# A decoder layer on one core: the output projection, the second norm and the FFN as one unrolled pipeline, and the attention outputs divided as they leave PSUM

## The chip, the core and the metric

One core of a Trainium2 chip runs the whole layer in one launch. The metric is device time in microseconds: the median of 3 runs is 2385.4 us (2385.02, 2385.40 and 2389.25 us).

## What is computed

Sixteen batches of 112 tokens, 256 wide (1792 tokens in all), go through a decoder layer with the norm after each part. The middle part is cross attention: 8 heads of width 128, with 375 keys in each batch, but heads are split off after batches and tokens are flattened, so every token sees all 6000 keys.

```python
x = layernorm(x + attn(x, Wq, Wk, Wv, Wo))            # 16 heads of 16, 4 key groups
q, k, v = split(x @ Wq), split(ctx @ Wk), split(ctx @ Wv)   # (8, 1792, 128), (8, 6000, 128)
sim = (q @ k.T) * 128 ** -0.5
mean = sim.mean(-1); sim = (sim - mean) * 1.5 + mean
out = merge(softmax(sim) @ v)                          # (1792, 1024)
x = layernorm(x + out @ Wout + bout)
h = gelu(x @ ternary(W1).T + b1)                       # exact gelu, 1024 wide
x = layernorm(x + h @ ternary(W2).T + b2)
```

Operands of the large products are kept as a high and a low float16 half, and a product is three matmuls (high by high, high by low, low by high); the ternary weights are exact and need two.

## The kernel before, in words

The program has three blocks (`with nc.Block()`), each with one instruction list per engine; at the end of a block all engines meet. Within a block every order and every wait is written out by hand: an instruction adds to a semaphore when it is done, and a list waits for a semaphore's value (`wait_ge`).

**Block 1, self attention and cross attention (lines 387 to 1274).** Cross attention runs over 56 groups `n` of 256 query tokens (8 heads by `NQB` = 7), each with 12 steps `s` of 512 keys. A step `f` is, on PE, the scores of step `f + LEAD` (`scores`, L404) and then the weighted sum of step `f` (`attend`, L428 to L432); on ACT, half of the casts of the exponentials (`exp_half`, L708), the copy of the scores into a ring (`keep_scores`, L701) and the exponential (`exp_full`, L718); on DVE, the subtraction of the row maximum (`subtract`, L879) and the running maximum (`running_max`, L858), which frees the two banks of the scores for PE; on POOL, the low half of the exponentials (L1201, L1203). `v` carries a column of ones, so that `attend` also sums the weights: a query tile has 129 columns in PSUM (`OW`), of which the last is its sum of weights. In step 1 of the next group ACT copies both query tiles of a group, 258 columns, to `o_buf` (`store_output`, L741), and SP writes them to DRAM (`store`, L1246), with the sums and undivided. `attend` of group `n` waits until group `n - 2` is copied.

**Block 2, output projection (lines 1287 to 1378).** It goes over 16 batches of 112 tokens, in loops with a body of two batches. SP loads a batch from DRAM into one of two buffers `raw` (8 heads by 129). DVE takes the reciprocal of the sums (L1302) and multiplies (L1305). PE turns the 8 heads (`transposes`, L1361), ACT and DVE split the result into halves (L1352 and `low`, L1311), PE multiplies by `Wout` (`project`, 24 matmuls, L1370), and DVE adds the residual (L1318) and collects statistics (L1321).

**Block 3, second norm, FFN and third norm (lines 1399 to 1545).** The statistics of all 16 batches are combined (L165, L167), ACT takes the roots (L174), and the FFN goes over 4 chunks of 448 tokens, three of them in a loop. For each of 8 parts `f` of the hidden layer PE does 4 matmuls (L1418), ACT does the gelu in float32 (L1442) and for even `f` again in float16 (L1447), for odd `f` DVE casts (L1505), and DVE makes the low half (L1507). Then PE does 16 matmuls for each batch (L1408), DVE adds the residual and collects statistics (L1471, L1475), and at the end of a chunk ACT takes a root (L1454) and DVE does the third norm (L1481 to L1490). The normalised and turned inputs of the next chunk (L179, L191, L197, L203) are made within the present one. SP stores two batches at a time (L1543). Roots and gelu need different tables on ACT, so each change is an `ACT_TABLE_LOAD`.

## Time and profile before

| | |
|---|---|
| median of 3 runs | 2385.4 us (2385.02 to 2389.25) |
| the profiled execution | 2389.25 us, span 2387.5 us |
| PE busy | 2296.9 us, 96% of the span |
| DVE busy | 2045.9 us, 86% |
| ACT busy | 1865.5 us, 78% |
| POOL busy | 1858.0 us, 78% |
| granted TensorE clock, mean | 0.991 |
| last matmul of block 1 starts | 2232.8 us from the start of the span |
| blocks 2 and 3 | the 154.5 us after that |

The span is the time from the first to the last instruction of one profiled execution; the rest of its 2389.25 us lies around it. The granted clock is a share of TensorE's full 2.4 GHz. A busy share is an average over stages with different limits, so the text reads stages apart. In rows of instructions, busy times of neighbours overlap; the distance from one start to the next is what an instruction costs its queue.

### The profile page before, as it was taken

The page shows a single profiled execution, that of the slowest core. Times are in us where ns is not written, and L with a number is a line of the kernel's source. Part 1 is how long each engine was busy: PE and PEld are TensorE (multiplying, and loading weights), DVE is VectorE, ACT ScalarE, POOL GpSimd, SP SyncE. Part 2 cuts the span into 40 slices and gives each one's busy share as a digit, 9 for nine tenths or more (in the row PEclk, how much of TensorE's full clock was granted, in tenths as well). Part 3 has the DMA queues.
Part 4 walks back from the last instruction along what each step waited for, and adds up shares of the span by engine and source line. Part 5 has one row for each costly group of instructions (what it writes and reads, how often), then busy time and mean ns, then how long its engine had stood idle before and what let it go on. Part 6 is the DMA issues. An engine that isn't in the chain of part 4 may idle for free. (4 is left out here: it accounts for less than half of the span.)

```text
span 2387.5 us, 67959 instructions
## 1 busy us (share of the span) xinstructions
PE 2296.9 (96%) x28874; PEld 2051.9 (86%) x28874; DVE 2045.9 (86%) x2237; ACT 1865.5 (78%) x2181; POOL 1858.0 (78%) x1110
## 2 busy tenths in 40 slices
PE   7988999999999999999999999999999999999787
PEld 3557998899989998999889988999899989998775
DVE  7878888988888888888878888888888888888776
ACT  4347888888888888888878888888888888888434
POOL 8744888888888898888878887889788888999101
PEclk9999999999999999999999999999999999999999
DMA  7401000000000000000000000000000000012211
GB/s 202 146 19 32 5 5 13 4 6 6 11 6 7 4 13 4 7 6 4 13 7 4 6 12 5 6 4 13 6 4 6 7 4 6 8 39 53 76 39 31
DMA packets 34869, 50.80 MB, mean 21 GB/s; under 512 B 2352, under 2 KB 27408, under 8 KB 34576
## 3 DMA queue, kind: packets, MB, share of 16 engines
q1 hardware_dynamic: 34576, 46.54, 6.7%
q8 instruction: 227, 3.72, 0.7%
q14 instruction: 66, 0.54, 0.1%
HBM read 31.01 MB, written 15.52 MB: 19 GB/s over the span
## 5 line engine op out<-in xcount | busy, mean ns | idle before, releaser
L1203 POOL TENSOR_TENSOR e_lo<-ring,e_hi 128x1024 f16<-128x1024 f32 (+1 forms) x665 | 1387.6, 2101 | 199.0 <-ACT ring L718 171.2
L858 DVE TENSOR_TENSOR run_max<-psum,run_max 128x1024 f16<-128x1024 f32 (+1 forms) x616 | 738.5, 1199 | 207.5 <-ACT ring L701 206.4
L701 ACT ACTIVATE ring<-psum 128x1024 f32<-128x1024 f32 (+1 forms) x672 | 674.3, 1004 | 198.8 <-PE psum L404 128.9
L879 DVE SCALAR_TENSOR_TENSOR ring<-ring,psum 128x1024 f32<-128x1024 f32 (+1 forms) x672 | 793.5, 1188 | 0.7 <-PE psum L636 0.7
L404 PE MATMUL psum<-qx_hi,k_hi 128*128 128x256 f16 x2632 | 717.9, 273 | 14.8 <-DVE run_max L858 5.9
L428 PE MATMUL psum<-v_main,e_hi 128*128 128x129 f16 x4032 | 718.2, 219 | 6.4 <-POOL e_lo L1203 6.4
L404 PE MATMUL psum<-qx_hi,k_lo 128*128 128x256 f16 x2632 | 717.7, 273 | 2.3 <-issue 2.3
L430 PE MATMUL psum<-v_main,e_hi 128*128 128x128 f16 x4032 | 718.7, 222 | 0.0
L404 PE MATMUL psum<-qx_lo,k_hi 128*128 128x256 f16 x2632 | 717.6, 273 | 0.0
L432 PE MATMUL psum<-v_main,e_lo 128*128 128x129 f16 x4032 | 716.7, 219 | 0.0
L718 ACT ACTIVATE ring<-ring 128x1024 f32<-128x1024 f32 (+1 forms) x672 | 696.4, 1036 | 1.3
L708 ACT ACTIVATE e_hi<-ring 128x1024 f16<-128x1024 f32 (+1 forms) x343 | 360.8, 1052 | 95.9 <-DVE ring L879 95.0
L1201 POOL CAST e_hi<-ring 128x1024 f16<-128x1024 f32 x329 | 334.2, 1016 | 120.6 <-ACT ring L718 117.2
L428 PEld LDWEIGHTS psum<-v_main,e_hi 128*128 128x128 f16 x4032 | 388.2, 96 | 14.5 <-POOL e_lo L1203 6.3
L432 PEld LDWEIGHTS psum<-v_main,e_lo 128*128 128x128 f16 x4032 | 398.4, 99 | 0.0
L430 PEld LDWEIGHTS psum<-v_main,e_hi 128*128 128x128 f16 x4032 | 391.3, 97 | 7.0
L404 PEld LDWEIGHTS psum<-qx_hi,k_hi 128*128 128x128 f16 x2632 | 257.2, 98 | 49.5 <-DVE run_max L858 13.6
L404 PEld LDWEIGHTS psum<-qx_hi,k_lo 128*128 128x128 f16 x2632 | 257.5, 98 | 30.3
L404 PEld LDWEIGHTS psum<-qx_lo,k_hi 128*128 128x128 f16 x2632 | 257.4, 98 | 27.1
L428 PE MATMUL psum<-v_tail,e_hi 128*128 128x129 f16 (+1 forms) x1232 | 219.8, 219 | 2.1 <-POOL e_lo L1203 2.1
L430 PE MATMUL psum<-v_tail,e_hi 128*128 128x128 f16 (+1 forms) x1232 | 220.1, 221 | 0.0
L432 PE MATMUL psum<-v_tail,e_lo 128*128 128x129 f16 (+1 forms) x1232 | 219.4, 218 | 0.0
(196 smaller groups left out, 2864.8 us busy)
## 6 DMA issues: line engine op xcount, KB each, us to landing
o_scratch<-o_buf SPq DMA_DIRECT2D x56, 129.0 KB, 2.9
raw<-o_scratch SPq DMA_DIRECT2D x16, 451.5 KB, 3.7
stage<-in_ctxT SPq DMA_DIRECT2D x6, 500.0 KB, 3.9
stage<-in_ctxT SPq DMA_DIRECT2D x12, 250.0 KB, 4.8
w_scratch<-wall SPq DMA_DIRECT2D x1, 2304.0 KB, 11.1
wall<-w_scratch SPq DMA_DIRECT2D x6, 384.0 KB, 4.1
x<-in_xT SPq DMA_DIRECT2D x4, 448.0 KB, 6.2
res<-in_x SPq DMA_DIRECT2D x1, 1792.0 KB, 15.5
```

The lines of the kernel that those rows point to most:

```text
L404: mm = pe.matmul(psum[:, 2 * (f % 2) + i // 2, (i % 2) * QB:(i % 2 + 1) * QB], lhsT=k[:, keys], rhs=q[:, qpar, :], start=(n == 0), stop=(n ...
L428: pe.matmul(out_t, lhsT=e_hi_f[keys, cols], rhs=v_f[keys, i, 0:OW], start=(s == 0 and i == 0 and t == 0), stop=False)
L430: pe.matmul(out_t[:, 0:DH], lhsT=e_hi_f[keys, cols], rhs=v_f[keys, i, OW:VW], start=False, stop=False)
L432: mm = pe.matmul(out_t, lhsT=e_lo_f[keys, cols], rhs=v_f[keys, i, 0:OW], start=False, stop=last_tile and t == QT - 1)
L701: a.activation(ring[:, f % SLOTS, 0:n], pair(f)[:, 0:n], ACT.Copy).then_inc(s_kept, 1)
L708: a.activation(e_hi[f % NEH][:, 0:n], ring[:, f % SLOTS, 0:n], ACT.Exp, scale=SIM_SCALE).then_inc(s_hi, 1)
L718: a.activation(slot, slot, ACT.Exp, scale=SIM_SCALE).then_inc(s_exp, 1)
L858: ins = v.tensor_tensor(run_max[:, 0:n], pair(f)[:, 0:n], run_max[:, 0:n], ALU.max)
L879: v.scalar_tensor_tensor(slot, slot, LIFT, psum[:, 6, 0:QB].unsqueeze(1).broadcast_to([P, t, QB]), ALU.add, ALU.subtract).then_inc(s_sub, 1)
L1201: g.tensor_copy(e_hi[f % NEH][:, 0:n], slot).then_inc(s_cast, 1)
L1203: g.tensor_tensor(e_lo[f % NEL][:, 0:n], slot, e_hi[f % NEH][:, 0:n], ALU.subtract).then_inc(s_lo, 1)
```

## The change

It has two parts.

**Division in block 1.** `o_buf` loses its column of sums. In step 1 of the next group DVE takes the reciprocal of both sums out of PSUM (`invert_sums`), and ACT copies the two tiles in two instructions with these as scale. The rows in DRAM are 128 columns for a head, and the reciprocal and the multiplication of block 2 are gone.

**One block in place of two.** Everything behind attention goes over 14 tiles of 128 tokens, not 16 batches of 112, without loops. `Wout`'s product, second norm, FFN and third norm of different tiles are interleaved by hand. There are 5 buffers `raw`; three loads are issued before the scores end and two right after. Residuals are added and evacuated two tiles at a time. The FFN has chunks of 4, 4, 4 and 2 tiles; `h32` has 3 buffers and `hT_hi` and `hT_lo` have 2; POOL takes the cast for odd `f` from DVE. PSUM: banks 0 and 1 for turned heads, 2 to 4 for the hidden layer, 5 for turned norms, 6 and 7 for both products.

```diff
-        raw = [at(VREG + r * 4128, f"raw{r}", [T, NH, OW], F32) for r in range(2)]
+        raw = [at(o, f"raw{r}", [P, NH, DH], F32)
+               for r, o in enumerate((VREG, VREG + 4096, WREG, KREG + 14336, KREG + 18432))]
...
                 def store_output(n):
-                    a.wait_ge(s_av, n * NGRP + NGRP)
+                    a.wait_ge(s_den, n + 1)
                     if n > 0:
                         a.wait_ge(s_od, n * 16)
-                    a.activation(o_buf[:, :, :], psum[:, 4 + n % 2, 0:QT * OW].rearrange(
-                        "p (t w) -> p t w", t=QT), ACT.Copy).then_inc(s_oev, 1)
+                    for t in range(QT):
+                        a.activation(o_buf[:, t, :], psum[:, 4 + n % 2, t * OW:t * OW + DH], ACT.Copy,
+                                     scale=o_den[:, t:t + 1]).then_inc(s_oev, 1)
...
+                def invert_sums(n):
+                    v.wait_ge(s_av, n * NGRP + NGRP)
+                    if n > 0:
+                        v.wait_ge(s_oev, n * QT)
+                    v.reciprocal(o_den[:, :], psum[:, 4 + n % 2, 0:QT * OW].rearrange(
+                        "p (t w) -> p t w", t=QT)[:, :, DH]).then_inc(s_den, 1)
...
                     ready = f + SUB_AHEAD
+                    if s == 1 and n > 0:
+                        invert_sums(n - 1)
...
                         sp.wait_ge(s_free, side_number(NBLK - 2, 0))
-                        for r in range(2):
-                            sp.wait_ge(s_od, (NBLK - NQB + 1) * 16)
-                            sp.dma_start(raw[r][:, :, :].rearrange("p h w -> p (h w)"),
-                                         o_part[r * T:(r + 1) * T, :]).then_inc(s_raw[r], 16)
+                        for i in range(3):
+                            load_tile(i)
                         sp.wait_ge(s_qk, NF_ALL)
...
+                        for i in range(3, NRAW):
+                            load_tile(i)
```

PE's list in the new block, with `up` the first product of the FFN for some `f` and `down` the second one for a pair of tiles:

```diff
+                pe.wait_ge(s_late, 48)
+                transposes(0)
+                for i in range(1, 6):
+                    transposes(i)
+                    project(i - 1)
+                transposes(6)
+                norm_transposes(0)
+                project(5)
+                transposes(7)
+                norm_transposes(1)
+                project(6)
+                for c in range(2):
+
+                    i = 4 * c + 8
+                    up(c, range(0, 4))
+                    transposes(i)
+                    project(i - 1)
+                    up(c, range(4, 8))
+                    transposes(i + 1)
+                    project(i)
+                    down(2 * c)
+                    if c == 0:
+                        transposes(i + 2)
+                    norm_transposes(2 * c + 2)
+                    project(i + 1)
+                    down(2 * c + 1)
+                    norm_transposes(2 * c + 3)
+                    if c == 0:
+                        transposes(i + 3)
+                        project(i + 2)
+                up(2, range(0, 4))
+                norm_transposes(6)
+                up(2, range(4, 8))
+                up(3, range(0, 8))
+                for p in range(4, 7):
+                    down(p)
```

The waits that matter there: `transposes(i)` for `low(i - 1)` (which frees banks 0 and 1), `project(i)` for `low(i)`, a part of `up` for the gelu three parts before it and for the low half of the normalised inputs of its whole chunk, the gelu for the low half three parts before it, `down(p)` for the low halves of its chunk.

**DVE in attention, step 1 of a group** (`qx_lo` is the low half of a later group's queries, `v_main` that of the values). Before:

```order
L846 SCALAR_TENSOR_TENSOR qx_lo<-psum,qx_hi 128x256
L879 SCALAR_TENSOR_TENSOR ring<-ring,psum 128x1024
L858 TENSOR_TENSOR run_max<-psum,run_max 128x1024
L879 SCALAR_TENSOR_TENSOR ring<-ring,psum 128x1024
L858 TENSOR_TENSOR run_max<-psum,run_max 128x1024
L879 SCALAR_TENSOR_TENSOR ring<-ring,psum 128x1024
L858 TENSOR_TENSOR run_max<-psum,run_max 128x1024
```

Now:

```order
L789 SCALAR_TENSOR_TENSOR qx_lo<-psum,qx_hi 128x256
L822 SCALAR_TENSOR_TENSOR ring<-ring,psum 128x1024
L801 TENSOR_TENSOR run_max<-psum,run_max 128x1024
L822 SCALAR_TENSOR_TENSOR ring<-ring,psum 128x1024
L801 TENSOR_TENSOR run_max<-psum,run_max 128x1024
L829 RECIPROCAL o_den<-psum 128x2
L822 SCALAR_TENSOR_TENSOR ring<-ring,psum 128x1024
L801 TENSOR_TENSOR run_max<-psum,run_max 128x1024
```

The reciprocal stands ahead of a subtraction and of a running maximum, once in each of the 56 groups. PE's and POOL's lists of attention are as before, and ACT's has two copies of 128x128 where one of 128x258 stood.

**DVE behind attention, from one chunk's last low half to the next chunk.** Before, the end of a chunk (`res` is the residual stream, `stats` and `meanvar` belong to the third norm):

```order
L1471 TENSOR_TENSOR res_71<-psum,res_71 112x256
L1475 BN_STATS stats_37325<-res_71 112x6
L1481 BN_AGGR meanvar_37326<-stats_37325 112x2 x4
L1482 ISA
L1483 TENSOR_SCALAR rstd_37327<-meanvar_37326 112x4
L1485 REGISTER_ALU
L1486 RECIPROCAL rstd_37327<-rstd_37327 112x4
L1487 REGISTER_ALU
L1490 TENSOR_SCALAR res_71<-res_71,meanvar_37326,rstd_37327 112x256 x4
```

Now, around the second chunk's low halves (`oT_lo` belongs to the projection, `bn`, `mean` and `inv` to the norms):

```order
L1538 BN_AGGR mean_37250<-bn_37248 128x2 x4
L1540 TENSOR_SCALAR inv_37252<-mean_37250 128x4
L1476 TENSOR_TENSOR oT_lo_37235<-psum,oT_hi_37233 128x1024
L1522 TENSOR_TENSOR hT_lo_37246<-h_2_37242,hT_hi_37244 128x512
L1522 TENSOR_TENSOR hT_lo_37246<-h_0_37240,hT_hi_37244 128x512
L1522 TENSOR_TENSOR hT_lo_37246<-h_1_37241,hT_hi_37244 128x512
L1522 TENSOR_TENSOR hT_lo_37246<-h_2_37242,hT_hi_37244 128x512
L1476 TENSOR_TENSOR oT_lo_37234<-psum,oT_hi_37232 128x1024
L1483 SCALAR_TENSOR_TENSOR res_74<-psum,res_74 128x512
L1487 BN_STATS bn_37247<-res_74 128x6 x2
```

The root of the third norm is no longer waited for in the place where it is asked for (L1540): the projection of later tiles and half of the next chunk's low halves stand between, and the cast has left the list.

## Rows read from the trace of the kernel before

**Rows 1.** Two stages: length, busy PE, PEld, DVE, ACT, POOL, then clock, DMA share, GB/s
```profile
320.00:1000.00 680.00, 676.25 (x8813) 622.33 (x8811) 599.89 (x587) 577.86 (x664) 578.12 (x336) 1.00 0.03 7
...
2233.00:2388.00 155.00, 122.99 (x928) 102.59 (x928) 111.00 (x250) 59.97 (x95) 12.18 (x16) 0.91 0.19 55
```
**Rows 2.** DVE and ACT in order of time, step 1 of a group in mid-attention
```profile
1129.38 1.23 DVE L858 TENSOR_TENSOR run_max<-psum,run_max 128x1024 f16<-128x1024 f32 x1 [0.24 <-ACT ring L701]
1130.52 1.21 DVE L879 SCALAR_TENSOR_TENSOR ring<-ring,psum 128x1024 f32<-128x1024 f32 x1
1132.19 1.23 DVE L858 TENSOR_TENSOR run_max<-psum,run_max 128x1024 f16<-128x1024 f32 x1 [0.45 <-ACT ring L701]
...
1132.99 0.38 ACT L741 ACTIVATE o_buf<-psum 128x258 f32<-128x258 f32 x1
1133.71 1.03 ACT L701 ACTIVATE ring<-psum 128x1024 f32<-128x1024 f32 x1 [0.33 <-POOL e_lo L1203]
```
**Rows 3.** PE's matmuls of that group's last keys: durations, first and last start
```profile
L432 PE MATMUL psum<-v_tail,e_lo x18: 217/218/222, 1119.9 to 1126.1; 128*128 128x129 f16 x16, 112*128 112x129 f16 x2
```
**Rows 4.** The turn from block 1 to block 2, by engine
```profile
2232.77 0.22 PE L432 MATMUL psum<-v_tail,e_lo 112*128 112x129 f16 x1
2236.12 0.96 PE L1361 MATMUL psum<-ident,o_sum 112*128 112x112 f32 x8 [3.13 <-DVE o_sum L1305]
...
2244.09 0.42 PE L1370 MATMUL psum<-wout_hi,oT_hi 128*112 128x256 f16 x1
...
2234.55 0.20 DVE L1302 RECIPROCAL rden_c<-raw 112x8 f32<-112x8 f32 x1 [3.39 <-PEq L387]
...
2233.03 0.39 ACT L741 ACTIVATE o_buf<-psum 128x258 f32<-128x258 f32 x1 [3.21 <-PE psum L432]
```
**Rows 5.** Block 2 in steady state, PE, DVE and ACT in order of time
```profile
2251.63 0.93 PE L1361 MATMUL psum<-ident,o_sum 112*128 112x112 f32 x8
2252.40 0.27 PE L1370 MATMUL psum<-wout_hi,oT_hi 128*112 128x256 f16 x1
...
2255.02 0.93 PE L1361 MATMUL psum<-ident,o_sum 112*128 112x112 f32 x8
...
2252.78 1.09 DVE L1311 TENSOR_TENSOR oT_lo<-psum,oT_hi 128x896 f16<-128x896 f32 x1
...
2255.22 0.92 ACT L1352 ACTIVATE oT_hi<-psum 128x896 f16<-128x896 f32 x1 [2.47 <-PE psum L1370]
```
**Rows 6.** Stretches of one microsecond; the granted clock is the third figure from the end
```profile
2237.00:2238.00 1.00, 0.63 (x4) 0.55 (x4) 0.39 (x1) 0.80 (x1) 0.00 (x0) 0.50 0.70 140
...
2247.00:2248.00 1.00, 1.00 (x10) 1.00 (x9) 0.00 (x0) 0.00 (x0) 0.00 (x0) 0.89 0.43 45
```
**Rows 7.** Groups of block 3: busy us, mean ns, idle time before them
```profile
L1408 PE MATMUL psum<-w12t,hT_hi 128*112 128x256 f16 x128 | 31.1, 286 | 5.1 <-DVE hT_lo L1507 5.0
L1418 PE MATMUL psum<-yT_hi,w12t 128*128 (+1 forms) x64 | 24.5, 382 | 7.2 <-ACT hT_hi L1447 6.1 <-DVE yT_lo L203 1.1
L1442 ACT ACTIVATE h<-psum,b1s 128x448 f32<-128x448 f32 x32 | 20.1, 635 | 5.3 <-PE psum L1418 2.6 <-DVE hT_lo L1507 2.2
L1507 DVE TENSOR_TENSOR hT_lo<-h,hT_hi 128x448 f16<-128x448 f32 x32 | 20.0, 629 | 7.1 <-ACT hT_hi L1447 6.3
```
**Rows 8.** ACT between two chunks, in order of time
```profile
2325.73 0.20 ACT L1454 ACTIVATE rstd<-rstd 112x4 f32<-112x4 f32 x1 [3.58 <-DVE rstd L1483]
2326.09 1.28 ACT L1442 ACT_TABLE_LOAD   x1 [0.16 <-issue]
2327.39 0.64 ACT L1442 ACTIVATE h<-psum,b1s 128x448 f32<-128x448 f32 x1
2327.92 0.63 ACT L1447 ACTIVATE hT_hi<-psum,b1s 128x448 f16<-128x448 f32 x1
```
**Rows 9.** The end: DVE's last group
```profile
2382.51 1.38 DVE L1490 TENSOR_SCALAR res<-res,meanvar,rstd 112x256 f32<-112x256 f32 x4
```

**Rows 10.** DMA issues of the page: count, size of one, us to landing
```profile
raw<-o_scratch SPq DMA_DIRECT2D x16, 451.5 KB, 3.7
```

More of the change, by code:

```diff
@@ new lines, in bank_of_projection, with bank_of_output, chunk_of, tiles @@
+        def bank_of_projection(p):
+            return 7 if p in (0, 2) else 6
+        def bank_of_output(p):
+            return 6 if p == 5 else 7
+        def chunk_of(i):
+            return i // 4
+        def tiles(c):
+            return range(FIRST[c], FIRST[c + 1])
+        def pairs_before(c):
+            return FIRST[c] // 2
+        def columns(c):
+            return (FIRST[c + 1] - FIRST[c]) * P
+        (t_tr, t_hi, t_lo, t_wp, t_n, t_cp, t_n3, t_add, t_nt, t_yh, t_yl, t_f1, t_ge, t_hh, t_hl, t_f2, t_add2,
+         t_bn, t_bn2, t_ag, t_sq, t_ag3, t_sq3, t_out) = [
+            sem("t_" + n) for n in ("tr", "hi", "lo", "wp", "n", "cp", "n3", "add", "nt", "yh", "yl", "f1", "ge",
+                                    "hh", "hl", "f2", "add2", "bn", "bn2", "ag", "sq", "ag3", "sq3", "out")]
@@ new lines, in _ @@
+                v.wait_ge(s_back, 16)
+                for i in range(2):
+                    low(i)
+                low(2)
+                residual(0)
+                low(3)
+                low(4)
+                residual(1)
+                statistics(0)
+                low(5)
+                norms(0)
+                low(6)
+                norm_low(0)
+                residual(2)
+                low(7)
+                norm_low(1)
+                hidden_low(0, range(0, 4))
+                low(8)
@@ new lines, in _ @@
+                residual(3)
+                statistics(1)
+                hidden_low(0, range(4, 8))
+                low(9)
+                norms(1)
+                second_residual(0)
+                low(10)
+                norm_low(2)
+                residual(4)
+                second_residual(1)
+                norm_low(3)
+                third_statistics(0)
+                low(11)
+                hidden_low(1, range(0, 4))
+                low(12)
+                residual(5)
+                statistics(2)
@@ new lines, in _ @@
+                hidden_low(1, range(4, 8))
+                low(13)
+                norms(2)
+                third_norms(0)
+                second_residual(2)
+                norm_low(4)
+                residual(6)
+                statistics(3)
+                second_residual(3)
+                norm_low(5)
+                third_statistics(1)
+                norms(3)
+                third_norms(1)
+                hidden_low(2, range(0, 4))
+                norm_low(6)
+                hidden_low(2, range(4, 8))
@@ L1531, in _ @@
+                hidden_low(3, range(0, 8))
+                second_residual(4)
+                second_residual(5)
+                third_statistics(2)
+                second_residual(6)
+                third_norms(2)
+                third_statistics(3)
+                third_norms(3)
             @block.gpsimd
             def _(g):
[L1533 to L1537 removed]
@@ L1539, in _, with keep @@
-            @block.sync
-            def _(sp):
-                with counted(sp, 0, NB, 2) as b:
-                    sp.wait_ge(s_n3, b + 2)
-                    sp.dma_start(out[bass.ds(b * T, 2 * T), :].rearrange("(i t) d -> t i d", t=T),
-                                 res2[:, bass.ds(b, 2), :]).then_inc(s_out, 16)
-                sp.wait_ge(s_out, NB * 8)
+                def keep(c):
+                    for i in tiles(c):
+                        g.wait_ge(t_n, i + 1)
+                        g.tensor_tensor(res2[:, i, :], norm2[i % 4][:, :], b2_b[:, :], ALU.add).then_inc(t_cp, 1)
@@ L1550, with cast @@
+                def cast(c, turns):
+                    n_cols = columns(c)
+                    for f in turns:
+                        turn = c * NF + f
+                        g.wait_ge(t_ge, turn + 1)
+                        g.tensor_copy(hT_hi[c % 2][:, f, 0:n_cols], h32[turn % 3][:, 0:n_cols]).then_inc(t_hh, 1)
+                g.wait_ge(s_b2, 16)
+                for c in range(4):
+                    keep(c)
+                    cast(c, (1, 3, 5, 7))
 def kernel(**inputs):
```

520 lines of the change are left out of this document (238 added, 282 removed).

## The prediction

> **What bounds the kernel now.** I first read busy time by stage. In 680 us of mid-attention PE is busy 676.25 us, while DVE has 599.89 and ACT 577.86 [rows 1]. PE is the bound there, and nothing the change does takes a matmul out of attention. In the 155 us behind it PE has 122.99 busy, with a mean clock of 0.91, and no other engine is full [rows 1]. That stage is bound by waits between engines and by PE's lower clock. These 154.5 us (2233.0, where the last matmul of attention ends, to 2387.5) are what the change can shorten.
>
> Next I read where they go. Between attention and the projection PE stops from 2233.0 to 2236.12: a block ends, then DVE divides [rows 4]. The projection then repeats every 3.39 us, 2251.63 to 2255.02: 8 transposes in 0.77 us and 24 matmuls in 2.62, or 0.109 us each [rows 5]. PE is full there. The FFN is not: the hidden layer's matmuls wait for the gelu, the gelu for matmuls and for low halves, the low halves for the gelu [rows 7]. Between chunks ACT waits for the third norm's statistics, takes a root, loads a table and only then starts the next chunk's gelu [rows 8].
>
> At full clock PE's own work behind attention is: 16 x 0.77 for transposes, 384 x 0.109 for `Wout`, 32 x 0.096 for the norm's transposes, 128 x 0.187 for the hidden layer (448 of the columns of which 256 cost 0.109, less a small fixed part) and 256 x 0.109 for the output. That is 109 us of the 154.5, so some 45 us are stalls, half clock, and both ends.
>
> **The tail after the change.** Work on PE first. Tiles of 128 tokens have the same 256 moving columns in `project` and `down`, so these cost per tile, not per token, and 14 tiles do what 16 batches did. `transposes`: 14 x 8 x 0.110 (0.096 x 128/112) = 12.3. `project`: 14 x 24 x 0.109 = 36.6. Norm transposes: 28 x 0.110 = 3.1. `up`: 24 parts of 512 columns at 0.863 and 8 of 256 at 0.437 = 24.2. `down`: 14 x 16 x 0.109 = 24.4. **The sum is 100.6 us.**
>
> *Start, 1.9 us.* DVE started 1.1 us behind the end of ACT's last copy [rows 4]. The last copy now comes behind a reciprocal (0.20, as L1302) and takes two instructions, so ACT ends about 0.35 later, at 2233.8, and PE starts at 2234.9. The division that stood between is gone.
>
> *Waits on PE, 8.4 us.* I walked the four lists of the new block against each other, each instruction starting when its queue is free and its waits are met. Durations are those of the rows, by the number of columns: ACT's copy of 1024 columns 1.02, DVE's `low` 1.22 with 1.14 from start to start (L858 has this size [rows 2]), a gelu 0.69 and 0.58 from start to start (448 columns: 0.64 and 0.53 [rows 8]), DVE's low half of 512 columns 0.70 (0.629 for 448 [rows 7]). PE waits 2.6 us before the second tile (copy, low half), since nothing else is ready. From then on `high` and `low` of a tile, 2.4 us with hand-over, fit beside a `project` of 2.6. The next large wait is 2.0 us before `up(2)`: the last pair of normalised tiles must be turned, copied and split. Chunks 2 and 3 have no projection to fill in, so three gelus for two parts (1.74 us) stand against 1.73 of PE, and for the narrow chunk 1.1 against 0.9: 3.2 us. Small ones add 0.6. In the walk DVE has 70 us of work in 110 and ACT 53, so neither is the bound. The cast for odd `f` is now POOL's, 0.62 us, beside DVE's work.
>
> *Half clock, 2.6 us.* Before, the clock fell from 2.4 to 1.2 GHz (0.50) in the microsecond from 2237, 4 us behind the end of attention, and came back at 2247, 3 us after the projections began at 2244.1 [rows 4, 6]. PE's early pause is shorter now but still there, so I keep the fall at 2237. The first `project` begins at about 2240, so I put the return at 2243.5. What runs from 2238.4 to 2243.5 takes twice its time, 2.6 us lost.
>
> *Behind PE, 8.5 us.* After the last `down`: residual and statistics of two tiles 1.7, four norms of the third chunk 1.6, statistics, root and inverse of the last two tiles 1.0, their norms 0.7. That is 5.0 us (before, it was 3.6). From the last norm's end (2383.9) to the end of the span it was 3.6 [rows 9], and stays.
>
> PE ends at 2234.9 + 100.6 + 8.4 + 2.6 = 2346.5, the span at 2355.0. **Against 2387.5 that is 32.5 us less.**
>
> One place in this sum is open to a rule. Between a root and the next gelu the trace shows a table load of 1.28 us, 0.16 us behind the root's end [rows 8], and the walk has 1.44 for each of the seven changes. The Trainium skill, page "ScalarE: Activation LUTs", section "What ACT_TABLE_LOAD costs", gives about 1.28 us plus 1.38 us of draining, 2.66 in all. By its figure the walk ends 2.4 us later; the rows show no such drain, and the row decides.
>
> **Loads.** 512 KB a tile instead of 451.5, every 3.4 us, landed in 3.7 before [rows 10]. Five buffers are filled ahead, so a load has over 10 us. I cost it at nothing. Only a landing time above that would show.
>
> **The division in attention.** DVE gets a reciprocal in each of 56 groups, 0.20 us (the nearest row has 8 numbers from SBUF, here 2 from PSUM [rows 4]). It stands ahead of a subtraction at 1130.52, and behind that DVE had 0.45 us of idle time before the next running maximum [rows 2]: covered. Its wait is met: the old group's last matmuls start by 1126.1 [rows 3], over 4 us before DVE comes. ACT's copy of 258 columns takes 0.38; two of 128 columns take somewhere between the same (if only columns cost) and twice that. The row behind it sat idle for 0.33 [rows 2], so most is covered, and PE is not waiting for ACT there. Per group the bounds are nothing below (no work leaves the loop) and 0.2 + 0.3 us above if DVE's and ACT's cover were gone, 0 to 28 us in all. I take 0, since PE is busy in 99% of this stage and both places have idle time of their own.
>
> So the profiled span would be 2355.0. The profiled execution, 2389.25 us, is the highest of the three; I take the difference of 32.5 us off the median, 2385.4, and round to **2353 us**.
>
> **Rivals.**
>
> *A. Part of the division shows (chance 0.09).* DVE and ACT are busy 88% and 85% of attention, and the three engines are coupled by banks and ring slots. If 0.2 us of each of 56 groups reaches PE, it is 11 us: 2364. For it: PE's releases come from DVE's running maximum. Against it: the idle time right behind both places.
>
> *B. The pipeline waits at its joints (0.14).* Before, the FFN's chunks waited for each other at every turn, and a hand-written order of lists can wait where a walk with mean durations does not. If the walk's 8.4 us of waits double, it is 2361.
>
> *C. The clock stays low for longer or falls again (0.12).* If it returns only at 2247 as before, 1.8 us more: 2355. If it also falls once in the thin stretch of chunks 2 and 3, 2 us more again: 2357.
>
> *D. Slower than before (0.03).* The reciprocal waits for the old group's last matmul, with running maxima queued behind it, which free the banks PE scores into. If DVE came there before PE was done, DVE would stand, then PE. The price decides from (32.5 + 4.8)/56 = 0.67 us a group: at 0.8 us it is 2353 + 45 = 2398. Against it stand the 4 us of margin [rows 2, 3].
>
> *E. The tail gains little, since raw tiles arrive late (0.02).* Then a tile costs its load of about 4.2 us (3.7 by size) instead of 3.4, at least 11 us for 14 tiles: 2364 or more.
>
> My forecast has 0.60. Its own range is 2349 (the gelu waits and half the others vanish) to 2357. To hold 8 in 10 I reach up to 2364, which takes in B, C and the first step of A, and down to 2348. Differences of under 0.2%, 4.8 us, can't be told from no change with this kernel. All cases but D and the far end of A lie below 2380.6: faster 0.95, within 0.2% 0.02, slower 0.03.
>
> **What would show it.** In the new profile: PE busy 98% or more in mid-attention still, attention's last matmul within 1 us of 2233; the first transpose at about 2235, and `project` from 2240; the projections 3.5 us apart; one wait of about 2 us before the third chunk's `up`; PE's last matmul near 2346.5 and the last norm 5 us behind. If the last matmul of attention ends later than 2236, the division was not covered (A or D). If it is on time and PE ends past 2351, the waits or the clock were mis-sized, and the idle time before PE's groups tells which (B or C).

## The result and the profile after

| | before | after |
|---|---|---|
| median | 2385.2 us (2384.53 to 2389.25, 4 runs) | **2356.0 us** (2354.88 to 2358.36, 4 runs) |
| ratio | | **0.9875**, 95% interval 0.9858 to 0.9892 |
| profiled execution, its span | 2389.25, 2387.5 us | 2358.36, 2356.6 us |
| last matmul of attention starts | 2232.77 us | 2235.13 us |
| from there to the end of the span ("the tail") | 154.7 us | 121.5 us |

The changed kernel is faster by 29.2 us between the medians; 2353 us had been forecast (ratio 0.9864, inside the interval). The tail fell by 33.2 us (it is counted here from the start of attention's last matmul; from its end, as in the prediction, it was 154.5 us before). Attention ended 2.4 us later in the profiled execution. Both differences have to be explained.

The stages first, as in [rows 1] (length, busy PE, PEld, DVE, ACT, POOL, clock, DMA share, GB/s):

```profile
320.00:1000.00 680.00, 676.35 (x8820) 622.54 (x8818) 601.14 (x606) 581.89 (x683) 577.93 (x335) 1.00 0.03 7
2233.00:2357.00 124.00, 107.14 (x869) 85.17 (x866) 78.78 (x169) 54.81 (x86) 21.46 (x30) 0.96 0.16 55
```

In mid-attention DVE and ACT have 1.3 and 4.0 us more to do than in [rows 1], and PE is busy for 676.35 us where it was 676.25. The second row still holds 2.3 us of attention. From the first transposes to the end of the last matmul PE was busy for 123.0 of 144.1 us before and is busy for 104.8 of 112.2 us now. So the 33.2 us are 18.2 less of PE's busy time, 13.7 less of its waits, and 1.3 at the start; behind PE nothing changed (7.2 and 7.1 us).

The turn, as in [rows 4] (start, duration, engine, line, operation, idle time before it and what ended it; PE, then DVE, then ACT):

```profile
2235.13 0.22 PE L374 MATMUL psum<-v_tail,e_lo 112*128 112x129 f16 x1
2237.21 1.25 PE L1304 MATMUL psum<-ident,raw 128*128 128x128 f32 x8 [1.86 <-PEq L329]
2241.05 1.94 PE L1304 MATMUL psum<-ident,raw 128*128 128x128 f32 x8 [2.59 <-DVE oT_lo L1476]
2242.78 0.42 PE L1316 MATMUL psum<-wout_hi,oT_hi 128*128 128x256 f16 x1
2246.38 1.04 PE L1304 MATMUL psum<-ident,raw 128*128 128x128 f32 x8
...
2235.39 0.17 DVE L829 RECIPROCAL o_den<-psum 128x2 f32<-128x2 f32 x1 [1.86 <-PE psum L374]
...
2235.59 0.62 ACT L684 ACTIVATE o_buf<-psum,o_den 128x128 f32<-128x128 f32 x2 [3.42 <-DVE o_den L829]
```

PE starts its transposes 2.08 us behind the start of attention's last matmul (3.35 before), waits 2.59 us for the first low half, and then has a tile every 3.5 us. The granted clock around it, by the microsecond, against [rows 6]:

```profile
2237.00:2238.00 1.00, 0.79 (x7) 0.82 (x8) 0.00 (x0) 0.00 (x0) 0.00 (x0) 0.97 0.45 131
2238.00:2239.00 1.00, 0.45 (x3) 0.06 (x1) 0.00 (x0) 0.45 (x1) 0.00 (x0) 0.50 0.06 16
...
2244.00:2245.00 1.00, 1.00 (x8) 0.73 (x6) 0.92 (x1) 0.05 (x1) 0.00 (x0) 0.61 0.63 193
2245.00:2246.00 1.00, 1.00 (x12) 0.90 (x10) 0.31 (x1) 0.00 (x0) 0.00 (x0) 1.00 0.77 315
```

It fell to half (1.2 GHz) at 2238, behind PE's 1.9 us of idle time and 0.8 us of transposes, and was back at 2.4 GHz within 2244, with the first projection at work. PE's waits from 2232 to the end (line that waits, what for, us in total, times, the longest):

```profile
PE psum L1339 <- ACT hT_hi L1435: 3.0, 5, 1.3
PE psum L1304 <- DVE oT_lo L1476: 2.6, 1, 2.6
PE psum L1304 <- PEq L329: 1.9, 1, 1.9
PE psum L1339 <- DVE yT_lo L1512: 1.7, 1, 1.7
```

These are the waits that the prediction had walked through: 2.6 before the second tile, 1.9 at the start, 1.7 before the third chunk (`up`, L1339), 3.0 for gelus in the last two chunks. No row has a wait for `raw`; a load of 512 KB landed in 3.6 us. The end on DVE, as in [rows 9]:

```profile
2349.47 0.69 DVE L1529 TENSOR_TENSOR res<-psum,res 128x512 f32<-128x512 f32 x1 [1.40 <-PE psum L1357]
...
2351.06 1.39 DVE L1549 TENSOR_SCALAR res<-res,mean,inv 128x256 f32<-128x256 f32 x4
...
2353.27 0.74 DVE L1549 TENSOR_SCALAR res<-res,mean,inv 128x256 f32<-128x256 f32 x2
```

The last norm ends at 2354.0, 4.6 us behind PE, and the span 2.6 us later.

### The profile page after: what moved, and what is told of

The parts are those of the page before. It is cut to its first block and busy times, and to the rows that moved or that the text cites. A ratio compares the mean times of both kernels' runs of the same rounds, so it can differ in the third digit from the quotient of the medians.

```text
span 2356.6 us, 67328 instructions
## 1 busy us (share of the span) xinstructions
PE 2281.6 (97%) x28774; PEld 2033.9 (86%) x28774; DVE 2016.9 (86%) x2210; ACT 1873.0 (79%) x2227; POOL 1866.2 (79%) x1124
```

## Experiments

All comparisons are with the kernel before on the same chip, whose medians there were 2386.7 to 2388.8 us. Because attention's end moves by up to 3.4 us from one execution to the next (below), I read the tail of each profile beside the medians. The tail has its own scatter: the two profiles of the changed kernel differ by 0.7 us, all of it busy time of PE (104.8 and 105.5 us), while its waits agree (7.4 us in both). Effects below 1 us are therefore read from waits and distances within a profile.

| kernel | median, us | ratio (95%) | last matmul of attention | tail, us |
|---|---|---|---|---|
| before | 2385.2 | 1 | 2232.77 | 154.7 |
| changed | 2356.0 | 0.9875 (0.9858 to 0.9892) | 2235.13 | 121.5 |
| changed, once more | 2356.3 | 0.9871 (0.9855 to 0.9886) | 2233.19 | 122.1 |
| division alone | 2385.6 | 0.9989 (0.9980 to 0.9998) | 2234.67 | 150.0 |
| division in the new block | 2360.9 | 0.9888 (0.9873 to 0.9903) | 2233.36 | 126.4 |
| five reciprocals | 2356.1 | 0.9866 (0.9850 to 0.9881) | 2231.70 | 122.5 |
| projection first | 2371.0 | 0.9932 (0.9918 to 0.9945) | 2231.88 | 136.5 |
| before, pauses filled | 2382.9 | 0.9977 (0.9968 to 0.9986) | 2231.98 | 148.2 |
| turn filled | 2353.5 | 0.9853 (0.9837 to 0.9868) | 2232.39 | 119.5 |
| end reordered | 2355.3 | 0.9860 (0.9845 to 0.9875) | 2232.41 | 120.6 |
| casts on DVE | 2355.6 | 0.9860 (0.9845 to 0.9875) | 2234.08 | 119.7 |
| combined | 2351.3 | 0.9850 (0.9835 to 0.9866) | 2231.88 | 117.2 |
| loop unrolled | 2349.6 | 0.9843 (0.9830 to 0.9857) | 2225.00 | 120.9 |
| combined and unrolled | **2343.8** | **0.9820** (0.9807 to 0.9833) | 2223.53 | 117.2 |

### Does the division cost anything in attention?

It was done alone, in three blocks as before:

```diff
                     for r in range(2):
-                        normalise(0, r)
...
-                    pe.wait_ge(s_on, b + (r + 1))
+                    pe.wait_ge(s_raw[r], b * 8 + 16)
...
+                    if s == 1 and n > 0:
+                        invert_sums(n - 1)
```

> The kernel before with the division alone: reciprocal and two scaled copies in attention, no reciprocal and no multiplication in block 2, everything else (16 batches of 112, three blocks) as before. My theory: the division is free in attention, since PE's transposes of the running maximum stood at the same distance (0.8 us) from those of before in all groups between 244 and 1189 us of the changed kernel. Then the last matmul of attention starts within 0.5 us of 2232.8, or later by what a longer spell at half clock after PE's one jump back at 1240 us costs (up to 2.5 us), block 2 starts about 1.0 us sooner behind it, its projections stay 3.39 us apart, and the median is about 2384.5 (-1 us). Rival A: 0.2 us in each of 56 groups reach PE, seen as a shift that grows by 5 us up to the middle of attention: about 2395.

Measured: ratio 0.9989, 2.6 us less with an interval from 0.5 to 4.8, where 1 us had been expected. PE's first transposes came 2.38 us behind attention's last matmul (3.35 before), so the start gained the 1.0 us expected, and the projections stayed 3.39 apart. The tail is 4.7 us shorter than before's, more than the division can give. Of the other 3.7 us, 2.6 are PE's busy time and 1.0 its waits. The busy time is the clock: before, it was at half for 10 us from 2301 and for 3 us in the last chunk, here for 7 us and not at all. The mean clock is the third figure from the end; before's rows first, then this kernel's:

```profile
2294.00:2314.00 20.00, 13.78 (x70) 8.21 (x68) 11.47 (x41) 8.76 (x15) 4.34 (x6) 0.74 0.00 1
2370.00:2378.00 8.00, 6.40 (x38) 5.60 (x38) 4.19 (x10) 2.97 (x4) 0.00 (x0) 0.79 0.00 0
```

```profile
2294.00:2314.00 20.00, 13.79 (x79) 8.69 (x78) 12.44 (x43) 9.42 (x17) 4.33 (x6) 0.83 0.00 1
2370.00:2378.00 8.00, 6.52 (x54) 5.77 (x54) 4.48 (x10) 2.06 (x3) 0.00 (x0) 1.00 0.00 0
```

The opposite: the changed kernel with the division taken out of attention again, so that DVE divides each tile in the new block.

```diff
+                def divide(i):
+                    x = raw[i % NRAW]
+                    v.wait_ge(s_raw[i % NRAW], 16 * (i // NRAW + 1))
+                    v.reciprocal(rden[:, i, :], x[:, :, DH]).then_inc(t_rd, 1)
+                    v.wait_ge(t_rd, i + 1)
+                    v.tensor_tensor(x[:, :, 0:DH], x[:, :, 0:DH],
+                                    rden[:, i, :].unsqueeze(2).broadcast_to([P, NH, DH]), ALU.mult).then_inc(t_div, 1)
```

> The changed kernel with the division taken back out of attention: one undivided copy with the sums, and DVE divides each tile of 128 tokens in the new block (reciprocal and one multiplication of 1024 columns, about 1.4 us, ahead of the low half of the tile before). My theory: the merged block gives nearly the whole gain, the division's place next to nothing. DVE has 14 x 1.4 = 20 us more, some 98 of 119 us, and PE starts about 1.0 us later behind attention: about 2357.5 (+1.5 against the changed kernel's 2356.0). Rival: the 2.4 us by which attention ends later in the changed kernel belong to the division; then the last matmul of attention starts at 2232.8 in this one, and the median is about 2355. Second rival: DVE's extra work turns up as waits of PE before each tile, at least 0.7 us each: 2366 or more.

Measured: 2360.9 us, tail 126.4, 4.9 longer than the changed kernel's. My 1.5 us was too low: it had the start, not the waits before tiles. The second rival had these waits, but at 0.7 us a tile or more, and they came before three more tiles only. PE's waits:

```profile
PE psum L1295 <- DVE oT_lo L1477: 5.4, 4, 2.5
PE psum L1330 <- ACT hT_hi L1426: 3.1, 5, 1.3
PE psum L1295 <- DVE raw L1470: 2.9, 1, 2.9
PE psum L1330 <- DVE yT_lo L1513: 2.6, 2, 1.7
```

Against the changed kernel's four that is 1.0 us more at the start, 2.8 before tiles and 0.9 before the hidden layer, 4.8 in all with 0.1 for gelus. DVE's 1.4 us for a division now stand in front of a low half, which fits them. So the new block needs DVE's time, and it is in attention that the division is cheap. How cheap, a larger dose shows:

```diff
+                    for i in range(4):
+                        v.wait_ge(s_more, 4 * n + i)
+                        v.reciprocal(o_more[i % 3][:, :], psum[:, 4 + n % 2, 0:QT * OW].rearrange(
+                            "p (t w) -> p t w", t=QT)[:, :, DH]).then_inc(s_more, 1)
```

> The changed kernel with a larger dose of what the division puts on DVE: four more reciprocals of the same sums in each of 56 groups, one waiting for the other, some 0.2 us each, and ACT's copies wait for the last of them. With one reciprocal the distance between the transposes of the running maximum at 245.2 and 1117.0 us was 871.8 us, as without. My theory: it is free because DVE has idle time behind that place, 0.45 us in the profile of the kernel before; 0.8 us more go past it, so a part shows, though PE has scores in reserve: 0 to 0.4 us a group, 871.8 to 881 us for these 24 and a half groups, and 2356 to 2378 us in all. Rival: the ring of scores gives a reserve of several us per group, and 0.8 us more cost nothing at all (871.8). Second rival: DVE's time comes on top in full: 0.8 a group, 891.4, and 2401 in all.

Measured: 2356.1 us, and 871.9 us between the two marks (243.37 to 1115.23), so the rival with the large reserve is right: four more reciprocals in each group cost attention nothing. They also stand behind the last group: PE's first transposes come 2.8 us behind the start of attention's last matmul instead of 2.1, and the tail is 122.5.

### Where do attention's 2.4 us come from?

The marks are the transposes of the running maximum (`transposes`, one pair a group). Those of the kernel before, then of the changed one:

```profile
244.38 0.28 PE L627 MATMUL psum<-ident,fold 128*128 128x128 f16 x2
1116.21 0.28 PE L627 MATMUL psum<-ident,fold 128*128 128x128 f16 x2
1410.33 0.28 PE L627 MATMUL psum<-ident,fold 128*128 128x128 f16 x2
2035.54 0.28 PE L627 MATMUL psum<-ident,fold 128*128 128x128 f16 x2
```

```profile
245.18 0.28 PE L569 MATMUL psum<-ident,fold 128*128 128x128 f16 x2
1116.96 0.27 PE L569 MATMUL psum<-ident,fold 128*128 128x128 f16 x2
1413.15 0.28 PE L569 MATMUL psum<-ident,fold 128*128 128x128 f16 x2
2038.05 0.28 PE L569 MATMUL psum<-ident,fold 128*128 128x128 f16 x2
```

The first two lie 871.83 and 871.78 us apart and the last two 625.2 and 624.9: no group is longer for its division. The changed kernel is 0.8 us late at the first of these marks (the first mark lay between 242.6 and 245.2 in fourteen profiles), and loses 2.1 between 1117 and 1413. There PE's only loop jumps back, at 1240 us, and PE stops twice with nothing to wait for. Before:

```profile
1241.15 0.28 PE L404 MATMUL psum<-qx_hi,k_hi 128*128 128x256 f16 x1 [2.69 <-issue]
1244.20 0.37 PE L404 MATMUL psum<-qx_hi,k_lo 128*128 128x256 f16 x1 [2.33 <-issue]
```

The changed kernel has the same stops, of 2.91 and 2.20 us. The clock falls in them. One row for 25 us around them, before, then the changed kernel:

```profile
1235.00:1260.00 25.00, 19.97 (x259) 18.44 (x256) 16.81 (x17) 17.09 (x20) 17.93 (x10) 0.93 0.03 8
```

```profile
1235.00:1260.00 25.00, 19.89 (x226) 17.64 (x224) 15.14 (x16) 16.06 (x20) 15.14 (x9) 0.80 0.03 8
```

A mean of 0.93 is 3.5 us at half clock, 0.80 is 10 us. The changed kernel was run again unedited:

> The changed kernel once more, nothing edited. Its first profile had a last matmul of attention 2.4 us later than the kernel before, of which 0.8 us arose ahead of cross attention and 2.0 us at 1240 us, where PE stops twice and the clock then stood at 0.50 for 10.6 us (3.2 us in the kernel before). My theory: both are chance of one execution, not the change: the distance of the running maximum's transposes from 245 to 1117 us is 871.8 us again, from about 1413 to 2038 it is 624.9, and the spell at half clock behind 1240 has another length, as it had in the other kernels with this same stretch (3 to 11 us). From attention's last matmul to the end: 121.5 us again. Rival: the change causes it, and the spell is 10 us again.

Measured: 2356.3 us; the marks were 871.9 us (244.96 to 1116.81) and 624.9 us (1411.08 to 2036.01) apart, the tail was 122.1, the stretch between 1117 and 1411 took 294.3 us instead of 296.2, and the spell was short:

```profile
1235.00:1260.00 25.00, 19.81 (x253) 18.28 (x251) 16.94 (x17) 17.29 (x21) 17.23 (x10) 0.93 0.03 8
```

Of the other kernels that have this stretch, the division alone had the long spell, the undivided one, the one with the end reordered and the one with casts on DVE a middle one (about 7 us), the rest the short one. So the 2.0 us are chance of one execution. The length of the spell does not set them by itself, though: the stretch took 293.9 to 294.3 us or 295.9 to 296.2, and the middle spell is found with both (294.3 with the undivided kernel, 296.0 and 295.9 with the other two). What does was not traced. Last, PE's loop was unrolled:

```diff
-                with pe.Fori(0, NH // 2 - 2) as pairs:
+                for pairs in range(NH // 2 - 2):
                     blocks(2 * NQB, 4 * NQB, pairs * 2)
```

> The changed kernel with PE's only loop unrolled: heads 2 and 3 and heads 4 and 5 have a list each, where a loop ran one list twice. At its jump back, at 1240 us, PE stops twice with no wait that the profile names (2.9 and 2.2 us), and half clock follows. My theory: the jump causes both stops (its code has to be fetched again), so they vanish and with them 3 to 11 us at half clock; the distance of the running maximum's transposes from 1117.0 to 1413.2 us, 296.2 us with the jump (294.1 at the shortest spell), goes to about 287.5, and the time falls by 6 to 9 us, to about 2348. Rival: the stops come from somewhere else in the program (a queue, an end of a block of code), and the longer list has them too: 294 to 296, 2356.

Measured: 2349.6 us, ratio 0.9843, and attention's last matmul at 2225.0. Both stops are gone, and with them the half clock:

```profile
1235.00:1260.00 25.00, 25.00 (x354) 23.90 (x352) 22.82 (x24) 23.09 (x29) 23.09 (x14) 1.00 0.02 7
```

From mark to mark it is 287.2 us (1116.13 to 1403.32), as expected. The loop's jump is the cause (or what else the loop brings at that place; the unrolling takes away both). The trace has a sign of the way it works. Queue 8 carries instructions in packets of 16 KB. From 1236 to 1248 us the changed kernel has three of them, the unrolled one has one (packets, MB, share of 16 engines; the changed kernel first):

```profile
q8 instruction: 3, 0.05, 1.9%
```

```profile
q8 instruction: 1, 0.02, 0.5%
```

Just before they came some 9 us apart, and in the unrolled kernel they go on so. With the jump one begins within 0.1 us of the first stop (1239.14 against 1239.21) and one 0.7 us ahead of the second (1242.69 against 1243.36); they take 1.4 us each, the stops 2.9 and 2.2. The Trainium skill, on the page "Runtime: NRT & Kernel Launch", section "Instruction fetch mechanics", says that a taken branch to code outside what has been fetched in sequence must have it fetched by DMA first. The trace agrees: an added fetch at each stop. What fills the rest of the stops was not traced.

### What did the new block's order bring?

The same instructions in one block, but projection first and then the FFN (PE's list; ACT's and DVE's follow it, and pairs of projections alternate between the two banks):

```diff
+                for i in range(1, NTL):
+                    transposes(i)
+                    project(i - 1)
+                project(NTL - 1)
+                norm_transposes(0)
+                norm_transposes(1)
+                for c in range(2):
+                    up(c, range(0, 8))
+                    down(2 * c)
+                    norm_transposes(2 * c + 2)
+                    down(2 * c + 1)
+                    norm_transposes(2 * c + 3)
```

> The changed kernel with the same instructions and tiles of 128, in one block, but in another order on PE, ACT and DVE: first all 14 tiles through the projection, then the FFN chunk by chunk, each chunk's eight parts in one go. It takes away only the interleaving of projection and FFN. The measure is the distance from the last matmul of attention to the end of the span: 154.7 us in the kernel before, 121.5 in the changed one. My theory: PE's own work (100.6 us) stays, and the waits that interleaving covered come back: about 2.7 us before the first part of the FFN (turn, copy, split), 1.5 us in and behind each of the first two chunks for gelus and low halves, 1.8 us before the second and third chunk, 8 us in all, and 1 to 3 us if the clock falls in them: a distance of 130 to 133, a time of about 2364 to 2367. Rival: the gain comes mostly from the interleaving; then the distance goes back to 145 or more, 2380. Second rival: interleaving is worth nothing (122, 2356).

Measured: 2371.0 us, tail 136.5. That is 15.0 us more than interleaved, where I had estimated 8 to 11. PE's largest waits:

```profile
PE psum L1339 <- DVE yT_lo L1492: 6.1, 3, 2.6
PE psum L1339 <- ACT hT_hi L1419: 3.0, 5, 1.3
PE psum L1357 <- DVE res L1509: 2.6, 2, 2.2
PE psum L1304 <- DVE oT_lo L1454: 2.6, 1, 2.6
PE psum L1357 <- DVE hT_lo L1502: 2.2, 4, 0.9
```

With 1.9 at the start and 1.5 before a norm's transposes they make 19.9 us against 9.2. What I had left out: `down` waits for the residual of the pair before it (2.6), and each of the first three chunks, not two, waits for its turned inputs. From the first transposes to the last matmul PE's busy time is 4.4 us longer too (109.2 against 104.8). A second spell at half clock, from 2294 to 2298 behind such a wait, is part of it; the rest was not traced further. Waits and busy time together are the 15 us. Of the tail's 33.2 us, 15.0 are thus the interleaving, in this one hand-written order without it, and 18.2 everything else: the division, one block instead of two, fewer, larger tiles, and what the profile of before had of half clock by chance. These were not told apart further.

### How much of it is clock?

The kernel before, with PE's pauses filled by matmuls that nobody reads (here those of block 2; others stand at the end of block 1 and around the first norm transposes):

```diff
                 pe.wait_ge(s_late, 48)
+                idle(13, 6)
                 for r in range(2):
                     transposes(0, r)
+                idle(30, 6)
```

> The kernel before with nothing changed but matmuls whose results nobody reads in PE's pauses: 18 of 128 columns behind the last matmul of attention, 13 of 256 columns at the start of block 2 and 30 behind the first two batches' transposes, 8 at the end of block 2, 22 at the start of block 3, and 9 behind each pair of the first four norm transposes. In the profile of the kernel before the clock was at 0.50 from 2237 to 2247, from 2301 to 2312 and from 2373 to 2376. My theory: a part of what the change gained is clock, since it has one long pause where the kernel before had three. Filled, the first two spells vanish: 3.2 us of doubled time in the first, 1 to 4 in the second (where ACT's gelus take over as the bound), so the distance from attention's last matmul to the end falls from 154.7 to about 149 us. Rival: the clock falls whatever runs there, or the added matmuls hold up what waits behind them: 154 to 158.

Measured: 2382.9 us, ratio 0.9977 (5.9 us less between the medians), tail 148.2 (expected 149), and the clock from 2233 to 2380 had a mean of 0.99, where it was 0.91 [rows 1]. So most of 6.5 us of the old tail were half clock behind pauses (the third, in the last chunk, had no filling and did not come here, as with the division alone); the changed kernel has one such pause left. Filling that one:

```diff
+                for _ in range(18):
+                    pe.matmul(psum[:, 6, 0:P], lhsT=ident16[:, :], rhs=ident16[:, :], start=True, stop=True)
...
                 transposes(0)
+                idle(22)
```

> The changed kernel with PE's pauses around the turn filled by matmuls whose results nobody reads: 18 of 128 columns behind the last matmul of attention (about 1 us) and 22 of 256 columns behind the transposes of the first tile (about 2.4 us, where PE waited 2.6 us). My theory: the fall of the granted clock to 0.50 from 2238 to 2244 comes from these pauses; filled, the clock stays at 1.00 and the 2.6 us that my prediction gave to it come back: about 2353.5, with the third tile's transposes at about 2244 in place of 2246.4. Rival: the pause at the block's end alone (2236.2 to 2237.2) or what is left makes the clock fall anyway; then the added matmuls run at half speed and hold up the second tile by about 2 us: 2358.

Measured: 2353.5 us, tail 119.5. The rows of PE at the turn:

```profile
2234.47 1.06 PE L1306 MATMUL psum<-ident,raw 128*128 128x128 f32 x8 [0.85 <-PEq L329]
2235.37 2.56 PE L1366 MATMUL psum<-wout_hi 128*128 128x256 f16 x22
2238.13 1.06 PE L1306 MATMUL psum<-ident,raw 128*128 128x128 f32 x8 [0.19 <-DVE oT_lo L1483]
2241.66 1.06 PE L1306 MATMUL psum<-ident,raw 128*128 128x128 f32 x8
```

The third tile begins 7.19 us behind the first, 9.17 in the changed kernel: 2.0 us. The granted clock was 1.00 in every microsecond until PE was done. The hole of 0.85 us that PE still had where the blocks meet brought no fall of the clock.

### Smaller places in the new block

DVE's list with the third chunk's norms one line earlier:

```diff
                 third_statistics(2)
+                third_norms(2)
                 second_residual(6)
-                third_norms(2)
                 third_statistics(3)
```

> The changed kernel with one line moved on DVE: the norms of the third chunk (reciprocal and four norms, 1.5 us) ahead of the last pair's residual, into 1.4 us in which DVE waits for PE. My theory: the chain behind PE's last matmul is DVE's own, so the last norm ends about 0.9 us sooner (residual 0.4 us late, 1.3 us of norms gone from the chain), about 2355.1 in all. Rival: the 2.6 us between the last norm and the end of the span hang on the stores of the third chunk, or the chain is ACT's root: no change, 2356.0.

Measured: 2355.3 us, tail 120.6. From the end of PE's last matmul to the end of the span it was 6.1 us, in both profiles of the changed kernel 7.1, so the order gave 1.0 us, where 0.9 had been expected (the medians alone could not tell it).

The casts for odd `f` back on DVE (and gone from POOL's list):

```diff
                         if f % 2:
+                            v.tensor_copy(hT_hi[c % 2][:, f, 0:n_cols], h32[turn % 3][:, 0:n_cols]).then_inc(t_hh, 1)
                             v.wait_ge(t_hh, turn // 2 + 1)
...
-                    cast(c, (1, 3, 5, 7))
```

> The changed kernel with POOL's 16 casts for odd f back on DVE. My theory: PE's waits of 3.0 us for the gelu in the last two chunks come in part from POOL, which casts in 0.6 to 1.1 us and stands 1.9 us in the second norm's additions at 2334.4 while a cast is due. DVE casts 512 columns in some 0.43 us and has room there (two low halves and a cast 1.65 us against 1.74 of three gelus), and in the first two chunks it has idle time: no gain and no loss but for the 1.3 us wait behind POOL's additions: about 2355. Rival: DVE's list is full around the chunks' ends (it is busy 79 of 124 us), and 6.9 us more of casts push the residuals and the next chunk's norms back: 2358 to 2360.

Measured: 2355.6 us (the medians do not tell it from the changed kernel), tail 119.7, 1.8 less than in the changed kernel's first profile. PE's wait for gelus fell from 3.0 us to this:

```profile
PE psum L1339 <- ACT hT_hi L1435: 1.2, 3, 0.5
```

The 1.8 us are in that one wait, so the part of the change that moves work to POOL costs time. In the changed kernel the first cast of the narrow chunk (128x256) stands behind two additions of the norm:

```profile
2333.33 1.13 POOL L1624 CAST hT_hi<-h 128x512 f16<-128x512 f32 x1 [0.74 <-ACT h L1431]
2334.43 1.85 POOL L1617 TENSOR_TENSOR res<-norm,b_b 128x256 f32<-128x256 f32 x2
2336.23 0.59 POOL L1624 CAST hT_hi<-h 128x256 f16<-128x256 f32 x1
```

### Put together

The turn filled, the end reordered, the casts on DVE, and the sixth pair's low half (`norm_low(5)`) ahead of the statistics of `second_residual(3)`:

> The changed kernel with what helped alone put together: PE's pauses around the turn filled by matmuls that nobody reads, the casts for odd f on DVE, the third chunk's norms ahead of the last pair's residual, and the low half of the sixth pair of normalised tiles ahead of the fourth pair's statistics. From attention's last matmul to the end it was 121.5 us; alone, the filled turn gave 2.0, the casts 1.8, the end's order 0.9, and the earlier low half should give 0.4 of PE's 1.7 us wait. My theory: they lie at different places and add up: 116.4 us, about 2351 in all. Rival: DVE's casts and its third norms meet at the end of the FFN, or DVE with the casts is late for the turn of a chunk: 118 or more, 2353.

Measured: 2351.3 us, tail 117.2, between the 116.4 expected and the rival's 118. PE waits 1.9 us for gelus and 1.4 for `yT_lo`: the low half moved ahead gave 0.3, and 0.7 of the casts' 1.8 us is not there in this mixture; which edit takes it was not traced.

> Both of the above: the four edits around and behind attention's end, and PE's loop unrolled. My theory: they don't touch each other, so the gains add: 116.4 us behind attention's last matmul, which starts some 6 to 8 us sooner: about 2343 to 2345. Rival: the stops at the jump stay (then as the combined kernel, 2351), or a longer list on PE stops elsewhere.

Measured: **2343.8 us**, ratio 0.9820 (0.9807 to 0.9833), tail 117.2, and attention's last matmul at 2223.5. The gains add. This version beats both kernels: 12 us below the changed one.

## Why the prediction came out as it did

- **Division in attention, costed at nothing: right.** The marks are as far apart with it as without, and 0.8 us more a group are free as well. Rivals A and D are out. D's price of 0.67 us a group, at which the gain would be gone, was never near: with some 0.9 us of reciprocals on DVE in each group, PE paid nothing. The reason given (idle time of 0.33 and 0.45 us behind both places) was too small a cover to explain that; what more covers it was not traced.
- **Its check failed all the same.** The last matmul of attention came at 2235.1, not within 1 us of 2233 as asked, though short of the 2236 that was named as the sign of A or D. The cause was what followed PE's jump, the stops and half clock (2.0 us more than in the kernel before), and a late start of the stage (0.8). A single time near the end of a long stage can't carry such a check; distances between marks within it can.
- **Start of PE.** 2.1 us from attention's last matmul to the first transposes were forecast, 2.08 measured.
- **PE's work and waits.** 111.6 us from first transpose to last matmul were forecast, 112.2 measured. That they agree so closely is in part luck, since three misses cancel. The waits were 7.4 (2.6, 1.7, 3.0 and 0.1 of small ones) and not 8.4 (2.6, 2.0, 3.2 and 0.6). Half clock cost 2.1 and not 2.6. But PE's work at full clock was 102.7 us (the filled turn: 105.2 us busy, less 2.6 of added matmuls) and not 100.6: 25.4 for `up` where 24.2 stood in the sum, and 0.2 or 0.3 more for each of the other four. B is out; but the 3.2 was not for the reason given: 1.8 of the measured 3.0 were POOL's, whose casts the walk had put beside DVE's work at no cost.
- **Half clock, 2.6 us.** The clock rose at about 2244.8 instead of 2243.5, with attention 2.4 us later. Filling the pauses gave 2.0 us back against the first profile of the changed kernel and 2.6 against the second.
- **Behind PE, 8.5 us.** It was 7.1: the norms 4.6 instead of 5.0, and 2.6 instead of 3.6 from the last norm to the end. The 3.6 had been carried over from the kernel before, and the change to other store sizes wasn't costed.
- **The sum.** The tail was forecast as 122.2 us and was 121.5 and 122.1. What failed in size is the last step, "I take the difference of 32.5 us off the median": the difference of the medians is 29.2. The profiled execution of before was the slowest of its four, and the one of after the slowest of its four too. The spread goes with the clock: in fifteen runs of the kernel before on one chip the mean granted clock is 0.992 in the fastest and 0.990 in the slowest, and in the changed kernel's four it is 0.995 in the fastest (span 2353.1) and 0.993 in the slowest (2356.6). In the profiles, before had 3 us at half clock in the last chunk that the division-alone profile lacked, and after had the long spell at 1240 us. In which stages a median run has its half clock was not measured. So C, the clock, cost no more than forecast in the new block; what it moved were the stages that had been taken as given.
- **The narrow range.** Its lower end, 2349, does not follow from its own terms: without the 3.2 us for gelus and half of the other 5.2 it is 2347. Nothing measured hangs on it.
- **Loads (E).** 512 KB landed in 3.6 us, and PE never waited for them.
- **The table load.** In the changed kernel too a gelu follows its load at once:

```profile
2324.22 0.20 ACT L1416 ACTIVATE inv<-inv 128x4 f32<-128x4 f32 x1 [1.47 <-DVE inv L1540]
2324.45 1.28 ACT L1431 ACT_TABLE_LOAD   x1
2325.74 0.69 ACT L1431 ACTIVATE h<-psum,b1s 128x512 f32<-128x512 f32 x1
```

The load is 1.28 us and begins when the root ends. The Trainium skill, page "ScalarE: Activation LUTs", section "What ACT_TABLE_LOAD costs", adds 1.38 us of draining; that part is not in these rows, and the measurement decides.

## What to carry to other kernels

Where an engine waits at joints between stages, add up three things: the waits, the half clock that follows PE's pauses, and the hand-over of blocks. Here filling the joints without any other change was worth 5.9 us by the medians (6.5 of the tail), interleaving two stages 15 of the tail's 33. Move small work into a stage where its engine has reserve, and test the reserve with a dose larger than the work. Compare stages by distances between marks, since one stop of PE 1000 us earlier can move everything behind it by 3 us.

## What was not expected of the hardware

- The jump back in PE's list stops PE twice, 5.0 us in all in the kernel before (2.69 and 2.33), and 3 to 10 us at half clock follow. Without the jump the same stretch is 9.0 us shorter than in the first profile of the changed kernel (287.2 against 296.2) and 6.9 shorter than in the kernel before (294.1).
- The same stop of the same code was followed by about 3, 7 or 10 us at 1.2 GHz in different executions.
- POOL and DVE lengthen each other: a POOL cast of 128x512 took from 0.61 to 1.13 us, the long ones beside DVE's low halves. Those low halves kept their time (0.68 to 0.69 us); but beside POOL's additions at 2334.4 one of 512 columns took 1.13 us, and one of 256 columns 0.94 where most took 0.41 to 0.43. The Trainium skill, page "SBUF — State Buffer", section "SBUF: two separate sides", has the two engines share a pair of ports that one of them holds for a whole instruction. The rows agree that they disturb each other; whether by whole instructions, they don't show.
